# Four PSUM banks for the second layer's sums, three for the first layer, one GpSimd block to a step, and four slots for g_full

## The chip, the cores and the metric

The kernel runs on one core of one Trainium2 chip. The metric is the time of one execution on the device, in microseconds (us). Three runs of the kernel before took 740.76, 741.46 and 741.74 us; their median is 741.46 us.

## What is computed

The reference is a "macaron" block: a feed-forward half (FFN), a gated linear recurrence (the mixer) and the same feed-forward half once more, on 8 sequences of 1024 rows with 256 features, all in float32. Cut to what matters:

```python
def ffn(x):                                   # x: (8, 1024, 256)
    h = layernorm(x) * gamma + beta
    y = silu(h @ dequant(fc1_q, fc1_scales) + fc1_bias)    # 256 -> 1024, scales by groups of 128 rows
    z = y @ dequant(fc2_q, fc2_scales) + fc2_bias          # 1024 -> 256
    return x + 0.5 * z
def mixer(x):
    a, c = sigmoid(x @ Wa + ba), tanh(x @ Wc + bc)
    b, d = x @ Wb + bb, x @ Wd + bd
    s[t] = a[t] * s[t-1] + (1 - a[t]) * b[t]               # over the rows of a sequence
    return (c * s) @ Wy + by + d
x = x + 0.5 * ffn(ln(x));  x = x + mixer(ln(x));  x = x + 0.5 * ffn(ln(x))
```

## The kernel before

The 8192 rows are cut into 16 tiles of 512 rows. The whole of x stays on chip in `resid`. Three phases follow each other: 16 tiles of the first FFN, 16 of the mixer, 16 of the second FFN. An FFN tile has eight steps, f = 0 to 7, one for each block of 128 hidden features. Every engine (PE is TensorE, ACT ScalarE, DVE VectorE, POOL GpSimd) runs its own list of instructions in program order, written out by hand step by step, and semaphores tie the lists together. In step f of a tile the engines do this:

- PE (`feed_forward` from L963): `half_products(f)` (two matmuls, the first 128 input features, into a bank of `ps_fc1`), `fc2` n = 0 of the group four steps back (two matmuls into a bank of `ps_z`; `LAG` is 4), `add_products(f-1)` (two matmuls, the other 128 input features, onto the half that has been scaled in place), `fc2` n = 1. In two of the steps (`TURN_AT`) `turn` (L889) follows, four transposes that bring one half of the next tile's `xhat` into `ps_tr`; in two others (`TURN_BACK_AT`) `turn_back` (L950), four transposes that bring z back. The two matmuls of a pair take the rounded value and its remainder (`h_hi` and `h_lo`, or `g_hi` and `g_lo`).
- ACT (from L574): `scale_half` for the f in `SCALED_ON_ACT`, `silu(f-1)` (the same bank read twice, into `g_full` and into `g_hi`), `round_h` after a turn, `first_sum` for the two sums of group 0, and one block of the layer norm (`normalise`, the block in `REST`) in step 7.
- DVE (from L702): `scale_half` for the other f, `add_group` (two additions of a PSUM bank onto `z_acc`, for groups 1 to 7), `lower_h` after a turn, `add_ffn` after a turn back, statistics (`STATISTICS_AT`) and variance.
- POOL (from L440): `g_low(f-1)` (L393: `g_lo` = `g_full` - `g_hi`) first in every step. Then, by tile position, `residual` (L384, four blocks that scale the next tile's `resid`), `rsqrt` (L342 to L366) for the tile after the next, and `normalise` (L374, three blocks of that tile's `xhat`; after the last one `xhat_ready` is raised).

The constants at L36 to L52 are tuples indexed by `before`, that is 0, 1 or 2 for tile 0, tile 1 and every later tile. In tiles 2 to 15 POOL does `residual` in step 1, `rsqrt` in step 2, `normalise` in steps 5 (two blocks) and 6 (one block); PE turns in steps 1 and 3 of the following tile. `turn(ln, ...)` waits for `xhat_ready` to reach ln + 1, and PE's whole list waits behind it. There is one `xhat` buffer and one `ps_tr` bank for the turns.

PSUM has eight banks of 128x512 float32. `ps_fc1` has four, used in turn (f % 4), so `half_products(f)` waits for `g_hi` of f - 4. `ps_z` has three, and the 16 sums of a tile go through them in turn (`BANKS`, L33), so a sum waits until the sum three before it has been added (`filled_before`, L244). `ps_tr` has one. `g_full` has two slots, so `silu(g)` waits for `g_low(g-2)` (L559); `g_hi` and `g_lo` have four slots and wait for `fc2` of g - 4.

## Time and profile before

| quantity | value |
|---|---|
| median of three runs | 741.46 us |
| the profiled execution | 739.66 us |
| its span, first to last instruction | 737.8 us |
| granted TensorE clock, mean | 0.998 |
| PE / PEld / DVE busy | 698.3 / 539.9 / 627.5 us |
| ACT / POOL busy | 637.0 / 623.6 us |
| busiest group on POOL: `g_lo` L393, 256 times | 329.5 us, 1293 ns each |
| busiest group on DVE: `z_acc` L690, 448 times | 322.5 us, 747 ns each |

PE counts the matmuls, PEld the loads of their weights, which overlap the matmuls. "Busy" is the time in which an engine had an instruction under way. The profiled execution lasted 1.86 us longer than its span, and its time is 1.8 us below the median of the three runs. The phases follow each other in the trace: the first FFN until about 305 us, the mixer until about 440 us, the second FFN until the end. In a timeline a line is: start in us, duration in us, engine, source line, operation, output<-inputs, shapes, count. Starts of neighbouring instructions may overlap, because the engines are pipelined; the distance between two starts is what an instruction costs its engine.

### The profile page before, as it was taken

To read this page: it belongs to the slowest core of one execution; us is meant where nothing else is said; L and a number is where in the kernel's file an instruction comes from. 1 tells how busy PE (TensorE), PEld (TensorE's weight loads), DVE (VectorE), ACT (ScalarE), POOL (GpSimd) and SP (SyncE) were. 2 spreads that over 40 slices of the span, in tenths; PEclk is the share of its full clock that TensorE was granted. 3 is DMA by queue.
4 is the path that set the end of the run, shared out by engine and by line. 5 is a ranking of instruction groups with operands and counts; after the bars stand their busy time and mean duration, and the time that the engine had idled before them with its cause. 6 is when DMAs were issued, how large, how long until landed. Compare 5 with 4: busy or idle time off the path is not lost. (4 is left out here: it accounts for less than half of the span.)

```text
span 737.8 us, 13716 instructions
## 1 busy us (share of the span) xinstructions
PE 698.3 (95%) x3250; PEld 539.9 (73%) x3250; DVE 627.5 (85%) x1216; ACT 637.0 (86%) x1052; POOL 623.6 (85%) x800
## 2 busy tenths in 40 slices
PE   4899999999999999989999997999999999999996
PEld 3577777777777777767788874777777777777774
DVE  6599998999999988688777785999999998999886
ACT  4889899998998999688888878889999899998984
POOL 5899999999999988767666658999999999999963
PEclk9999999999999999999999999999999999999999
DMA  8640000000000000000000000001110000000001
GB/s 259 205 140 1 1 0 0 0 0 0 0 0 0 1 1 0 1 1 1 0 0 0 1 0 1 2 28 35 44 37 28 28 29 28 28 30 28 30 30 59
DMA packets 19674, 19.96 MB, mean 27 GB/s; under 512 B 1532, under 2 KB 19378, under 8 KB 19634
## 3 DMA queue, kind: packets, MB, share of 16 engines
q1 hardware_dynamic: 19536, 19.48, 8.3%
q8 instruction: 16, 0.26, 0.1%
q14 instruction: 24, 0.20, 0.1%
q10 hardware_dynamic: 98, 0.02, 0.0%
HBM read 11.11 MB, written 8.39 MB: 26 GB/s over the span
## 5 line engine op out<-in xcount | busy, mean ns | idle before, releaser
L690 DVE SCALAR_TENSOR_TENSOR z_acc<-ps_z,cols,z_acc 128x512 f32<-128x512 f32 x448 | 322.5, 747 | 55.2 <-PE ps_z L902 24.5
L393 POOL TENSOR_TENSOR g_lo<-g_full,g_hi 128x512 fp32r<-128x512 f32 x256 | 329.5, 1293 | 36.2 <-ACT g_hi L562 35.4
L902 PE MATMUL ps_z<-g_hi,q_sb 128*128 128x512 f32 x512 | 210.8, 412 | 16.1 <-ACT z_acc L552 8.4
L560 ACT ACTIVATE g_full<-ps_fc,safe_scale 128x512 f32<-128x512 f32 x256 | 178.6, 698 | 51.9 <-PE ps_fc L902 38.6
L902 PE MATMUL ps_fc<-h_hi,q_sb 128*128 128x512 f32 x512 | 215.1, 420 | 4.8 <-ACT ps_fc L545 4.1
L902 PE MATMUL ps_fc<-h_lo,q_sb 128*128 128x512 f32 x512 | 203.6, 398 | 0.0
L902 PE MATMUL ps_z<-g_lo,q_sb 128*128 128x512 f32 x512 | 202.1, 395 | 0.0
L562 ACT ACTIVATE g_hi<-ps_fc,safe_scale 128x512 fp32r<-128x512 f32 x256 | 178.5, 697 | 0.0
L902 PEld LDWEIGHTS ps_z<-g_hi,q_sb 128*128 128x128 f32 x512 | 96.0, 187 | 69.5 <-ACT z_acc L552 22.4
L545 ACT ACTIVATE ps_fc<-ps_fc,bias,ratio 128x512 f32<-128x512 f32 x160 | 122.2, 764 | 1.4 <-DVE bias L785 1.4
L902 PEld LDWEIGHTS ps_fc<-h_hi,q_sb 128*128 128x128 f32 x512 | 97.2, 190 | 25.8 <-ACT ps_fc L545 4.1
L902 PEld LDWEIGHTS ps_z<-g_lo,q_sb 128*128 128x128 f32 x512 | 96.4, 188 | 19.1
L902 PEld LDWEIGHTS ps_fc<-h_lo,q_sb 128*128 128x128 f32 x512 | 97.6, 191 | 17.2
L670 DVE TENSOR_SCALAR ps_fc<-ps_fc,ratio,bias 128x512 f32<-128x512 f32 x96 | 77.9, 811 | 4.5 <-PE ps_fc L902 4.5
L360 POOL TENSOR_TENSOR rstd<-var_terms,minus_half 128x8 f32<-128x8 f32 (+1 forms) x48 | 69.6, 1451 | 4.0
L384 POOL TENSOR_SCALAR resid<-resid,res_scale,shift 128x256 f32<-128x256 f32 x128 | 69.3, 555 | 0.8 <-ACT xhat L528 0.8
L651 DVE BATCH_NORM_STATS2 stats<-resid 128x6 f32 (+1 forms) x192 | 67.0, 410 | 1.8 <-DMA resid<-in_L_attn_x 1.8
L1018 PE MATMUL ps_fc<-wd_sb,q_int 128*128 128x256 f32 x240 | 56.7, 379 | 0.0
L528 ACT ACTIVATE xhat<-resid,shift,rstd 128x256 f32 (+1 forms) x96 | 52.2, 591 | 4.0 <-POOL shift L366 3.9
L374 POOL TENSOR_SCALAR xhat<-resid,rstd,shift 128x256 f32<-128x256 f32 x96 | 53.4, 562 | 0.1
L895 PE MATMUL ps_tr<-ident,xhat 128*128 128x128 f32 x320 | 48.6, 275 | 3.0 <-ACT xhat L528 1.5
L895 PEld LDWEIGHTS ps_tr<-ident,xhat 128*128 128x128 f32 x320 | 39.6, 141 | 14.9 <-issue 4.0
(105 smaller groups left out, 813.8 us busy)
## 6 DMA issues: line engine op xcount, KB each, us to landing
resid<-in_L_attn_x SPq DMA_DIRECT2D x15, 512.0 KB, 4.2
out_x<-resid SPq DMA_DIRECT2D x15, 512.0 KB, 2.9
q_int<-in_L_ffn_fc_q SPq DMA_DIRECT2D x4, 512.0 KB, 7.0
...
```

Of the source, the lines that this page charges most:

```text
L360: nc.gpsimd.tensor_tensor(rstd[:, 0:n, :], var_terms[:, 0:n, :], minus_half[:, 0:n, :], ALU.pow).then_inc(rstd_ready, 1)
L384: last = nc.gpsimd.tensor_scalar(resid[:, t, a, :], resid[:, t, a, :], res_scale[:, a:a + 1], shift[:, 1, a:a + 1], ALU.mult, ALU.add)
L393: nc.gpsimd.tensor_tensor(g_lo[:, g % 4, :], g_full[:, g % 2, :], g_hi[:, g % 4, :].bitcast(F32), ALU.subtract).then_inc(g_ready, 1)
L545: nc.scalar.activation(bank, bank, ACT.Identity, bias=bias[:, f:f + 1], scale=ratio[:, f:f + 1]).then_inc(scaled_on_act, 1)
L560: nc.scalar.activation(g_full[:, g % 2, :], bank, ACT.Silu, scale=scale)
L562: nc.scalar.activation(g_hi[:, g % 4, :], bank, ACT.Silu, scale=scale).then_inc(g_hi_ready, 1)
L651: last = nc.vector.bn_stats(stats[:, a, :], resid[:, t, a, :])
L670: nc.vector.tensor_scalar(bank, bank, ratio[:, f:f + 1], bias[:, f:f + 1], ALU.mult, ALU.add).then_inc(scaled_on_dve, 1)
L690: nc.vector.scalar_tensor_tensor(out=z, in0=bank_of(g, n, par), scalar=col(R_S2 + KC * g + n), in1=z, op0=ALU.mult, op1=ALU.add).then_inc( ...
L895: last = nc.tensor.transpose(bank[:, a * P:(a + 1) * P], xhat[:, a, c * P:(c + 1) * P], ident[:, :])
L902: last = nc.tensor.matmul(out, w, v, start=start and i == 0, stop=stop and i == len(pairs) - 1, skip_group_check=not start)
L1018: nc.tensor.matmul(mix_bank(t, par, half)[:, a * D:(a + 1) * D], xn[:, par, k, at:at + P], wd_sb[:, k, :], start=False, stop=False, skip_g ...
```

## The change

`ps_fc1` gets three banks and `ps_z` four. The sums of the second layer use bank 2 * (g % 2) + n, so a sum waits for the addition of group g - 2 with the same n. The first layer's banks follow the list `FC1_BANKS`; where a bank comes again after two steps (f = 1 of even tiles, f = 7 of odd tiles), `half_products` is issued after `add_products` (`HALF_LATE`). `g_full` gets four slots. The constants move work between steps: POOL's four `residual` blocks go to steps 0 to 3, `rsqrt` to step 4, the three `normalise` blocks to steps 5, 6 and 7; PE's turns of tiles 2 to 15 go to steps 0 and 2, its turns back to 4 and 5, with `round_h`, `lower_h` and `add_ffn` moved to match; the variance goes to step 7; ACT scales f = 1, 3, 5, 6, 7 and DVE f = 0, 2, 4; both first sums are issued in step 4. No arithmetic is added or removed. The mixer's banks get other numbers. The diff, cut to its core:

```diff
-    BANKS = tuple(tuple((FC * KC * par + KC * g + n) % 3 for g in range(FC)) for par in range(2) for n in range(KC))
-    SCALED_ON_ACT = (0, 2, 4, 5, 6)
-    SCALED_ON_DVE = (1, 3, 7)
+    FC1_BANKS = (0, 1, 2, 0, 1, 2, 0, 1, 2, 0, 1, 2, 0, 1, 2, 1)
+    HALF_LATE = ((1,), (7,))
+    SCALED_ON_ACT = (1, 3, 5, 6, 7)
+    SCALED_ON_DVE = (0, 2, 4)
     TINY = 2.0 ** -60
     STATISTICS_AT = 4
-    VARIANCE_AT = 5
-    RESIDUAL_AT = (4, 1, 1)
-    RSQRT_AT = (5, 2, 2)
-    NORMALISE_AT = ((6, 7), (5, 6), (5, 6))
-    TURN_AT = ((3, 5), (1, 3), (1, 3))
-    TURN_OUT_AT = ((3, 5), (1, 3), (1, 3))
-    H_LOWER_AT = ((4, 6), (2, 4), (2, 4))
-    XN_LOWER_AT = (4, 6)
-    FIRST_SUM_AT = (4, 5)
-    TURN_BACK_AT = ((), (5, 6), (5, 6))
-    ADD_AT = ((), (6, 7), (6, 7))
+    VARIANCE_AT = 7
+    RESIDUAL_AT = ({2: (0, 1), 3: (2, 3)},) + ({0: (0,), 1: (1,), 2: (2,), 3: (3,)},) * 2
+    RSQRT_AT = (5, 4, 4)
+    NORMALISE_AT = ({6: (0, 1), 7: (2,)},) + ({5: (0,), 6: (1,), 7: (2,)},) * 2
+    TURN_AT = ((3, 5), (1, 3), (0, 2))
+    TURN_OUT_AT = ((3, 5), (1, 3), (0, 2))
+    H_LOWER_AT = ((4, 6), (2, 4), (1, 3))
+    XN_LOWER_AT = (3, 5)
+    TURN_BACK_AT = ((), (5, 6), (4, 5))
+    ADD_AT = ((), (6, 7), (5, 6))
...
-        g_full = sb("g_full", [P, 2, TILE])
+        g_full = sb("g_full", [P, 4, TILE])
...
-        ps_fc1 = ctx.enter_context(nc.psum_tensor("ps_fc1", [P, 4, TILE], F32))
-        ps_z = ctx.enter_context(nc.psum_tensor("ps_z", [P, 3, TILE], F32))
+        ps_fc1 = ctx.enter_context(nc.psum_tensor("ps_fc1", [P, 3, TILE], F32))
+        ps_z = ctx.enter_context(nc.psum_tensor("ps_z", [P, 4, TILE], F32))
         ps_tr = ctx.enter_context(nc.psum_tensor("ps_tr", [P, TILE], F32))
-        ps_tr2 = ps_z[:, 2, :]
+        ps_tr2 = ps_z[:, 3, :]
         back_banks = (ps_tr[:, :], ps_fc1[:, 0, :])
-        ps_ab = ps_z[:, 0, :]
-        ps_c = ps_z[:, 1, :]
+        ps_ab = ps_z[:, 1, :]
+        ps_c = ps_z[:, 2, :]
+        ps_mix = ((ps_fc1[:, 0, :], ps_fc1[:, 2, :]), (ps_fc1[:, 1, :], ps_z[:, 0, :]))
...
+        def fc1_bank(f, par):
+            return ps_fc1[:, FC1_BANKS[FC * par + f], :]
+        def silu_before(f, par):
+            here = FC * par + f
+            return next(k for k in range(1, FC) if FC1_BANKS[here - k] == FC1_BANKS[here])
+        def bank_of(g, n):
+            return ps_z[:, KC * (g % 2) + n, :]
+        def filled_before(g, n, ff):
+            if g == 2:
+                return z_begun[n], ff + 1
+            if g > 2:
+                return z_added[n], (FC - 1) * ff + (g - 2)
+            return z_added[n], (FC - 1) * ff + (g - 1)
...
+            def normalise(ln, t, blocks, complete):
                 if blocks[0] == 0:
                     pool.wait_ge(shift_ready, ln + 1)
@@ -373,24 +382,26 @@
                 for a in blocks:
                     last = nc.gpsimd.tensor_scalar(xhat[:, a, :], resid[:, t, a, :], rstd[:, 0, a:a + 1],
                                                    shift[:, 0, a:a + 1], ALU.mult, ALU.add)
-                if last_part:
+                if complete:
                     last.then_inc(xhat_ready, 1)
-            def residual(ln, t, shares):
-                pool.wait_ge(xhat_ready, ln + 1)
-                wait(pool, xhat_half_ready, shares)
-                for a in range(SUB):
+            def residual(ln, t, shares, blocks=range(SUB)):
+                if blocks[0] == 0:
+                    pool.wait_ge(xhat_ready, ln + 1)
+                    wait(pool, xhat_half_ready, shares)
+                for a in blocks:
                     last = nc.gpsimd.tensor_scalar(resid[:, t, a, :], resid[:, t, a, :], res_scale[:, a:a + 1],
                                                    shift[:, 1, a:a + 1], ALU.mult, ALU.add)
-                last.then_inc(resid_scaled, 1)
+                if blocks[-1] == SUB - 1:
+                    last.then_inc(resid_scaled, 1)
...
-                        if behind >= 1 and f == RESIDUAL_AT[before]:
-                            residual(ln + 1, t + 1, share(ln + 1, ff0))
+                        if behind >= 1 and f in residual_at:
+                            residual(ln + 1, t + 1, share(ln + 1, ff0), residual_at[f])
                         if behind >= 2 or ff0 == 0:
                             t2, twice = (t + 2, True) if behind >= 2 else (1 - behind, False)
                             if f == RSQRT_AT[before]:
                                 rsqrt(ln + 2, twice, share(ln + 1, ff0))
                             if f in normalise_at:
-                                normalise(ln + 2, t2, MOST[normalise_at.index(f)], f == normalise_at[1])
+                                normalise(ln + 2, t2, normalise_at[f], f == FC - 1)
...
-                wait(act, g_ready, FC * ff + (g - 1))
-                nc.scalar.activation(g_full[:, g % 2, :], bank, ACT.Silu, scale=scale)
+                wait(act, g_ready, FC * ff + (g - 3))
+                nc.scalar.activation(g_full[:, g % 4, :], bank, ACT.Silu, scale=scale)
...
-                        if f == FIRST_SUM_AT[1]:
-                            first_sum(ff, par, 1)
                         if f in SCALED_ON_ACT:
-                            scale_half(ff, f)
+                            scale_half(ff, f, par)
+                        if f == LAG:
+                            first_sum(ff, par, 0)
                         if f >= 1:
                             silu(ff, f - 1, par)
...
-                        if f == FIRST_SUM_AT[0]:
-                            first_sum(ff, par, 0)
+                        if f == LAG:
+                            first_sum(ff, par, 1)
...
-                wait(pe, g_hi_ready, FC * ff + (f - 3))
-                products(ps_fc1[:, f % 4, :], [(w[:, 0, f * P:(f + 1) * P], h[:, par, 0, :])
+                wait(pe, g_hi_ready, FC * ff + (f + 1 - silu_before(f, par)))
+                products(fc1_bank(f, par), [(w[:, 0, f * P:(f + 1) * P], h[:, par, 0, :])
...
-                        half_products(ff, ln, f, par)
+                        if f not in HALF_LATE[par]:
+                            half_products(ff, ln, f, par)
...
+                        if f in HALF_LATE[par]:
+                            half_products(ff, ln, f, par)
```

## Rows read from the trace of the kernel before

**Rows 1.** Page, busy time by engine, and the last chain by line.

```profile
PE 698.3 (95%) x3250; PEld 539.9 (73%) x3250; DVE 627.5 (85%) x1216; ACT 637.0 (86%) x1052; POOL 623.6 (85%) x800
...
POOL g_lo L393 14%; POOL rstd L360 3%; POOL resid L384 3%; POOL xhat L374 3%; PE ps_z L902 2%; PE ps_fc L902 2%; DVE z_acc L690 0%; POOL neg_mean L357 0%; POOL var_terms L353 0%; POOL var_terms L351 0%; PE ps_tr L959 0%; POOL shift L366 0%;
```

**Rows 2.** Windows over tiles 2 to 14; columns: stretch, length, engines, clock, DMA.

```profile
56.60:268.91 212.31, 207.45 (x961) 160.64 (x960) 193.80 (x361) 193.36 (x316) 197.92 (x252) 1.00 0.00 0
484.21:695.97 211.76, 207.27 (x961) 160.76 (x960) 191.81 (x352) 192.65 (x313) 198.19 (x253) 1.00 0.09 30
```

**Rows 3.** Timeline of PE, one steady tile of the second FFN.

```profile
474.25 0.40 PE L902 MATMUL ps_fc<-h_lo,q_sb 128*128 128x512 f32 x1
474.91 0.50 PE L902 MATMUL ps_z<-g_hi,q_sb 128*128 128x512 f32 x1 [0.27 <-ACT z_acc L552]
475.25 0.40 PE L902 MATMUL ps_z<-g_lo,q_sb 128*128 128x512 f32 x1
...
476.16 0.39 PE L902 MATMUL ps_fc<-h_lo,q_sb 128*128 128x512 f32 x1
...
477.03 0.40 PE L902 MATMUL ps_z<-g_lo,q_sb 128*128 128x512 f32 x1
...
479.32 0.40 PE L902 MATMUL ps_z<-g_lo,q_sb 128*128 128x512 f32 x1
...
483.51 0.40 PE L902 MATMUL ps_fc<-h_lo,q_sb 128*128 128x512 f32 x1
```

**Rows 4.** Timeline of PE: turns (tiles 1, 2, 14, mixer; then 1, 2, 14).

```profile
38.95 0.66 PE L895 MATMUL ps_tr<-ident,xhat 128*128 128x128 f32 x4
...
56.60 0.60 PE L895 MATMUL ps_tr<-ident,xhat 128*128 128x128 f32 x4
...
268.91 0.60 PE L895 MATMUL ps_tr<-ident,xhat 128*128 128x128 f32 x4
...
303.62 0.60 PE L895 MATMUL ps_tr<-ident,xhat 128*128 128x128 f32 x4
...
466.59 0.63 PE L895 MATMUL ps_tr<-ident,xhat 128*128 128x128 f32 x4
...
484.21 0.60 PE L895 MATMUL ps_tr<-ident,xhat 128*128 128x128 f32 x4
...
695.97 0.60 PE L895 MATMUL ps_tr<-ident,xhat 128*128 128x128 f32 x4
```

**Rows 5.** Timeline of POOL, the same steady tile.

```profile
471.11 1.31 POOL L393 TENSOR_TENSOR g_lo<-g_full,g_hi 128x512 fp32r<-128x512 f32 x1
...
475.35 2.54 POOL L393 TENSOR_TENSOR g_lo<-g_full,g_hi 128x512 fp32r<-128x512 f32 x2
...
480.42 1.30 POOL L393 TENSOR_TENSOR g_lo<-g_full,g_hi 128x512 fp32r<-128x512 f32 x1
481.71 0.56 POOL L374 TENSOR_SCALAR xhat<-resid,rstd,shift 128x256 f32<-128x256 f32 x1
482.23 1.30 POOL L393 TENSOR_TENSOR g_lo<-g_full,g_hi 128x512 fp32r<-128x512 f32 x1
```

**Rows 6.** Timelines of ACT and POOL: the way to POOL, and first_sum.

```profile
484.03 0.69 ACT L560 ACTIVATE g_full<-ps_fc,safe_scale 128x512 f32<-128x512 f32 x1 [0.23 <-PE ps_fc L902]
484.61 0.68 ACT L562 ACTIVATE g_hi<-ps_fc,safe_scale 128x512 fp32r<-128x512 f32 x1
...
485.37 1.29 POOL L393 TENSOR_TENSOR g_lo<-g_full,g_hi 128x512 fp32r<-128x512 f32 x1 [0.20 <-ACT g_hi L562]
...
491.94 1.45 ACT L552 ACTIVATE z_acc<-ps_z,cols 128x512 f32<-128x512 f32 x2
```

**Rows 7.** Timeline of POOL, the shorter rsqrt of tile 14, first FFN.

```profile
273.69 1.29 POOL L393 TENSOR_TENSOR g_lo<-g_full,g_hi 128x512 fp32r<-128x512 f32 x1
...
276.86 2.53 POOL L393 TENSOR_TENSOR g_lo<-g_full,g_hi 128x512 fp32r<-128x512 f32 x2
```

**Rows 8.** Window with PE idle, start of second FFN (columns as rows 2).

```profile
448.00:450.00 2.00, 0.08 (x1) 0.08 (x1) 1.96 (x7) 1.85 (x4) 2.00 (x4) 1.00 0.00 0
```

More of the change, by code:

```diff
@@ L57, in macaron_kernel @@
     out_view = out.rearrange("b s d -> (b s) d").rearrange("(t a p) d -> p t a d", p=P, a=SUB)
-    MOST, REST = (range(0, 2), range(2, 3)), range(3, 4)
+    REST = (3,)
     R_S1, R_B1 = 0, KC * FC
@@ L133, in macaron_kernel @@
         xn_hi, xn_lo = h_hi, h_lo
-        c_sb, state = g_full[0:N, :, :], z_acc[0:N, 0, :, :]
+        c_sb, state = g_full[0:N, 0:2, :], z_acc[0:N, 0, :, :]
         scratch = q1_int[:, :, :].bitcast(F32).rearrange("p k f -> p (k f)").rearrange("p (b n) -> p b n", n=TILE)
@@ L239, in scaled_count @@
             return len(where) * ff + (where.index(f) + 1)
-        def bank_of(g, n, par):
-            return ps_z[:, BANKS[2 * par + n][g], :]
-        def filled_before(bank, g, n, ff, par):
-            here = [(j, m) for j in range(FC) for m in range(KC)]
-            before = here[:here.index((g, n))] if g < FC else here
-            for back, uses, p in ((0, before, par), (1, here, 1 - par)):
-                for j, m in reversed(uses):
-                    if BANKS[2 * p + m][j] == bank:
-                        if j == 0:
-                            return z_begun[m], ff - back + 1
-                        return z_added[m], (FC - 1) * (ff - back) + j
+        def fc1_bank(f, par):
[11 more added lines that the diff above has]
+            return z_added[n], (FC - 1) * ff + (g - 1)
         def share(ln, ff0):
@@ L264, in mix_bank @@
             if type(t) is int and t == NT - 1:
-                return ps_z[:, half, :]
-            return ps_fc1[:, 2 * par + half, :]
+                return ps_z[:, 1 + half, :]
+            return ps_mix[par][half]
         halves = (range(0, SUB // 2), range(SUB // 2, SUB))
@@ L551, in first_sum @@
                 wait(act, back_done, 2 * ff - 2)
-                nc.scalar.activation(z_acc[:, par, n, :], bank_of(0, n, par), ACT.Identity,
+                nc.scalar.activation(z_acc[:, par, n, :], bank_of(0, n), ACT.Identity,
                                      bias=col(R_B2 + n), scale=col(R_S2 + n)).then_inc(z_begun[n], 1)
             def silu(ff, g, par):
-                step, bank, scale = FC * ff + g, ps_fc1[:, g % 4, :], safe_scale[:, g:g + 1]
+                step, bank, scale = FC * ff + g, fc1_bank(g, par), safe_scale[:, g:g + 1]
                 act.wait_ge(fc1_done, step + 1)
-                wait(act, g_ready, FC * ff + (g - 1))
-                nc.scalar.activation(g_full[:, g % 2, :], bank, ACT.Silu, scale=scale)
+                wait(act, g_ready, FC * ff + (g - 3))
+                nc.scalar.activation(g_full[:, g % 4, :], bank, ACT.Silu, scale=scale)
                 wait(act, fc2_done, 2 * step - 6)
@@ L668, in scale_half @@
                     dve.wait_ge(bias_ready, 1)
-                bank = ps_fc1[:, f % 4, :]
+                bank = fc1_bank(f, par)
                 nc.vector.tensor_scalar(bank, bank, ratio[:, f:f + 1], bias[:, f:f + 1], ALU.mult,
@@ L936, in fc2 @@
                     pe.wait_ge(g_ready, FC * ff + (g + 1))
-                bank = bank_of(g, n, par)
-                wait(pe, *filled_before(BANKS[2 * par + n][g], g, n, ff, par))
+                bank = bank_of(g, n)
+                wait(pe, *filled_before(g, n, ff))
                 at = slice(n * P, (n + 1) * P)
```

31 lines of the change are left out of this document (14 added, 17 removed).

## The prediction, made before the result was known

> **What bounds the kernel now.** I read the page's busy times first, then windows, then the timeline of one steady tile. No engine stands out: PE has 95%, the other three 85 or 86% [rows 1]. The chain that ended last runs through POOL more than through any other engine, mostly `g_lo` [rows 1]. The windows give the rate. In the second FFN the first turns of tiles 2 and 14 are 211.76 us apart [rows 2, 4], so 12 tiles take 17.65 us each; in the first FFN it is 17.69. In one such tile PE is busy 17.3 us, POOL 16.5, ACT 16.1 and DVE 16.0 (rows 2 divided by 12). For PE that number says little, because the shown durations overlap; I count issue slots. From 479.32 to 483.51 there are 18 slots, 0.233 us each. Four transposes cost 0.44 us: 475.25 to 476.16 is 0.91 and holds two slots beside them [rows 3]. A tile has 64 products and four groups of transposes: 64 x 0.233 + 4 x 0.44 = 16.7 us. So PE loses 0.95 us per tile, in small waits on banks and on `g_lo`. Between 474.25 and 475.25 it loses 1.00 - 0.47 = 0.53 us, waiting for a first sum; between 476.16 and 477.03 another 0.40 [rows 3].
>
> **The order that matters here: xhat to turn.** In the kernel before, the last POOL block of `xhat` ends at 482.27 (start 481.71, 0.56 us) and the first turn of the next tile starts at 484.21 [rows 4, 5]. The turn is 1.94 us later than it would have to be. That block stands in POOL's step 6 and the turn at the end of PE's step 1. The change puts them in POOL's step 7 and at the end of PE's step 0: two steps of PE nearer, 2 x 8 x 0.233 = 3.7 us and a group of transposes where one lies between. 1.9 us of slack can't pay for that. This decides the forecast, so I work out the loop that it closes.
>
> **The new loop.** Let a tile's first turn start at 0. PE's list from there to the end of `add_products(3)` in step 4 is fixed: the turn (0.44), steps 1, 2 and 3 with 24 products, the second turn (0.44), and in step 4 `half_products(4)`, `fc2` and `add_products(3)`, 6 products: 30 x 0.233 + 0.88 = 7.9 us. Nothing can overtake, as the list is in order. ACT then has to finish `first_sum(0)`, which it now issues before `silu(3)`: it can start two slots (0.47) before the end of `add_products(3)` and takes 0.73 (1.45 for two, rows 6), so it adds some 0.2. From a finished `add_products` to the start of `g_low` on POOL it takes 1.6 us: the last product's slot ends at 483.74, `silu` is read twice by ACT, and `g_lo` starts at 485.37 [rows 3, 6]. So POOL starts `g_low(3)` at 9.7. Behind it in POOL's list stand `rsqrt`, now in step 4, then `g_low(4)`, a block, `g_low(5)`, a block, `g_low(6)`, the last block. From `g_lo` through `rsqrt` to the next `g_lo` POOL takes 475.35 - 471.11 = 4.24 us, and a `g_lo` with one block takes 482.23 - 480.42 = 1.81 [rows 5]: 4.24 + 3 x 1.81 + 0.1 for the end of the last block and the signal = 9.8. The next turn can't start before 9.7 + 9.8 = 19.5; I take 19.4, since `silu` was reached a little late in the row used. PE by itself would be there at 16.7, so it stands still for 2.7 us in each tile, at one place. All its small waits are hidden in that one.
>
> **The edits, one by one.** (1) Four `ps_z` banks and the earlier `first_sum` take away the waits on z sums, part of the 0.95 us; with PE stalled 2.7 us elsewhere they give nothing in tiles 2 to 14 and about 0.5 us in each tile where no turn waits. (2) Three `ps_fc1` banks: `half_products(f)` now waits for `silu(f-3)`, which by the 1.6 us above is done about a step before. Cost nothing while ACT has room, which it has (16.1 of 19.4 us). (3) The two late `half_products` give the scaling on ACT less time: it starts two product pairs later, and `silu` behind it starts up to 0.7 us later. It falls on f = 1 or 7, not on the path through `silu(3)`; nothing. (4) Four slots of `g_full` take ACT's wait for POOL away. That wait holds ACT up behind POOL's `rsqrt` now; in the loop above no ACT wait is left to remove. (5) `residual` one block to a step: the same four blocks; they lie before `g_low(3)`, where POOL has time. `g_low` and a block take 1.81 us a step and PE's steps 1.87 or 2.3, so `g_low(3)` isn't late. (6) The moved turns back, `add_ffn`, variance and DVE's scalings: DVE has 16.0 us of work in 19.4 and each addition waits for PE; nothing. The one tight place is the second turn, two steps behind the first, which needs `lower_h` of the first; these stood two steps apart before too, and the distance is the same. I allow 0 to 0.3 us a tile there. Before these edits no row shows a tile with a turn that waits, so the bounds of the per-tile cost are the one-path value of the second rival below (+0.15) and 19.4 + 0.3 (+2.05); I take 19.4, as each of its terms is a measured distance.
>
> **The sum,** on the profiled execution. First FFN: tile 0 has its `residual` earlier, which can save POOL up to 1 us before its last `xhat` block; I take 0.5, so the first turn of tile 1 moves from 38.95 [rows 4] to 38.4. That turn stays in step 1, one step (1.87) later in the list than in later tiles: to the first turn of tile 2 it is 19.4 - 1.87 = 17.6 us, at 56.0. Then 12 intervals of 19.4: tile 14's turn at 288.8, where it was at 268.91. `rsqrt` of tiles 14 and 15 has fewer operations: from `g_lo` to `g_lo` 276.86 - 273.69 = 3.17 [rows 7], 1.07 less, so tile 15's turn comes 18.3 later. Tile 15's own `xhat` has two `xn_low` of about 1.3 us (as a `g_lo`) between the `g_low`s, of which one and a half lie on the path: 20.3. The mixer's first turn comes at 327.4 in place of 303.62 [rows 4]: +23.8. The mixer keeps its work and order; a bank wait at its start goes, -0.4. Second FFN: tile 1's turn from 466.59 to 466.59 + 23.4 - 0.7 = 489.3, tile 2's at 506.9, tile 14's 232.8 later at 739.7, where it was at 695.97: +43.7. From there to the end PE runs unstalled; it has one step more to do (+1.9) and loses three small waits (-1.5). Together +44 us: the profiled execution goes from 739.66 to about 783.8, and the median, which lies 1.8 above it, from 741.46 to 785.5.
>
> **Rivals.** (a) The change does what its parts are for: no turn waits, the z waits are gone, and the tile falls to what POOL and PE need, 16.85 us. That gives 25 x 0.8 + 4 = 24 us less, 717. It is faster, and decides if `xhat` is complete 2.7 us earlier than I work out, that is if `rsqrt` and the three blocks lie beside PE's steps 5 to 0. For it: POOL's 16.5 us fit. Against it: even without `rsqrt`, the last block needs `add_products(6)` of step 7, 1.6 us to POOL, a `g_lo` and a block: 1.4 + 1.6 + 1.81 = 4.8 us after step 7 began, and the turn is due after 3.7. (b) The loop closes only by that last path: `rsqrt` is absorbed, and a tile takes 16.7 + 1.1 = 17.8 us: +0.15 a tile, 25 tiles and 1.3 us at the start of each FFN give 747. Against it is that POOL's list has no way around `rsqrt`. (c) PE's stall of 2.7 us brings the clock down to its lower level behind each stall: with 4 us of a tile's path at half speed, 2 us more a tile, 835. Against it: PE stood still for nearly all of 448 to 450 us and the granted clock read 1.00 [rows 8]; it is 1.00 in the steady stretches too [rows 2]. (d) Small waits add up to 0.5 us a tile in the loop: 797.
>
> The Trainium skill's page "TensorE: Matmul & The Clock Gate", section "HAM oscillation — how this bites in real kernels", says that a matmul engine with long enough idle gaps goes back to the throttled clock; by it rival (c) would hold if the gaps here were long enough, and the row of 448 to 450 us doesn't show it. The page "Perfetto Trace Analysis", section "Optimization Strategy", says that the same gap coming back on the engine that should be saturated can mean too little PSUM for the next tile; by it the fourth `ps_z` bank is the cure and rival (a) the outcome. PE's wait for a first sum agrees with it, but the fourth bank doesn't reach the new wait.
>
> **How the numbers follow.** Forecast 785.5 with chance 0.79; (a) 0.06, (b) 0.04, (c) 0.03, (d) 0.08. Uncertainty of the forecast itself: 0.35 us a tile over 25 tiles is 9 us, and 3 us for the starts and ends, so 773 to 798, which takes in (d); this is the range for 8 in 10. A change of 0.2% is 1.5 us, about what a measurement can tell from none. Faster is (a), 0.06; within 0.2% 0.01; slower 0.93.
>
> **What would show it.** If right: first turns of tiles 2 to 14 are 19.4 us apart; PE idle for 2.5 to 3 us just before each, released by POOL's `xhat`; POOL without idle time from `g_low(3)` to the last block; no PE wait on `z_acc` in these tiles. Three loop terms can be read off alone: 7.9, 1.8 and 9.8. If turns start without a wait, or the tile takes less than 17.7 us, the loop is wrong. If the tile is longer than 19.8, look at `lower_h` before the second turn, or at the clock.

## The result, and the profile after

The changed kernel took 813.47 us (median of four runs, 813.15 to 813.73) beside 741.6 us before: a ratio of 1.097, with a 95% interval of 1.0951 to 1.0989. It is slower, as forecast, but by 72 us where 44 were forecast, and it lies 15.5 us above the upper end of the range. The profiled execution took 813.32 us, with a span of 811.5 us.

The page of the changed kernel: busy time by engine, then the chain that ended last, by engine and by line.

```profile
PE 718.2 (89%) x3250; PEld 557.2 (69%) x3250; DVE 626.9 (77%) x1216; ACT 643.0 (79%) x1052; POOL 624.9 (77%) x800
...
PE 22%; POOL 13%; issue 5%; DVE 1%; POOLq 0%; DVEq 0%; ACT 0%
PE ps_z L913 9%; PE ps_fc L913 9%; POOL g_lo L404 6%; POOL xhat L383 2%; PE ps_tr L906 2%; POOL rstd L369 2%; POOL resid L394 1%; PE ps_tr L970 1%; POOL neg_mean L366 0%; POOL shift L375 0%; POOL var_terms L360 0%; POOL var_terms L362 0%; D
```

POOL and DVE are as busy as before in us (624.9 and 626.9), and less in share; PE shows 20 us more than in [rows 1], for the same 3250 instructions. Two things are to be seen already: no engine has more work, so time was lost in waits, and something made the same matmuls longer.

The windows over tiles 2 to 14 of both FFNs, from first turn to first turn (stretch and length; busy us and count for PE, PEld, DVE, ACT, POOL; granted clock; DMA share):

```profile
58.33:304.76 246.43, 218.37 (x961) 169.97 (x961) 191.88 (x360) 196.04 (x315) 198.43 (x252) 0.94 0.00 0
523.29:769.01 245.72, 216.54 (x960) 168.81 (x961) 190.55 (x351) 195.18 (x312) 198.47 (x253) 0.95 0.08 26
```

Twelve tiles take 246.43 and 245.72 us where [rows 2] has 212.31 and 211.76: 20.5 us a tile. And the granted clock is 0.94 and 0.95, where it was 1.00. A mean hides how that is spread, so I read the first turns one by one. The timeline of PE, three first turns that follow each other (start, duration, engine, line, output<-inputs, shapes, count, and in brackets the idle time before it with its releaser):

```profile
160.64 1.03 PE L906 MATMUL ps_tr<-ident,xhat 128*128 128x128 f32 x4 [2.49 <-POOL xhat L383]
...
181.75 0.65 PE L906 MATMUL ps_tr<-ident,xhat 128*128 128x128 f32 x4 [2.21 <-POOL xhat L383]
...
201.28 0.73 PE L906 MATMUL ps_tr<-ident,xhat 128*128 128x128 f32 x4 [2.48 <-POOL xhat L383]
```

PE stands still 2.2 to 2.5 us before each, and POOL's `xhat` ends it, as forecast. But the intervals are 21.11 and 19.53 us, and these are the two kinds there are: of the 24 intervals between tile 2 and tile 14 in the two FFNs, 9 are 19.5 to 19.7 us and 15 are 20.8 to 21.2 us. The windows of one us just after a turn of a long interval, and just after one of a short interval, show the difference (columns as above):

```profile
161.00:162.00 1.00, 1.00 (x6) 0.90 (x5) 0.00 (x0) 0.21 (x1) 1.00 (x2) 0.50 0.00 0
162.00:163.00 1.00, 1.00 (x4) 0.81 (x3) 0.00 (x0) 0.92 (x2) 0.28 (x1) 0.50 0.00 0
163.00:164.00 1.00, 1.00 (x3) 0.75 (x3) 0.49 (x1) 0.32 (x1) 0.00 (x0) 0.50 0.00 0
164.00:165.00 1.00, 1.00 (x5) 0.83 (x4) 0.49 (x2) 0.65 (x2) 0.00 (x0) 0.91 0.00 0
165.00:166.00 1.00, 1.00 (x6) 0.79 (x5) 1.00 (x2) 0.62 (x2) 0.30 (x1) 1.00 0.00 0
...
182.00:183.00 1.00, 1.00 (x8) 0.87 (x7) 0.01 (x1) 0.47 (x1) 1.00 (x2) 1.00 0.00 0
183.00:184.00 1.00, 1.00 (x6) 0.82 (x5) 0.74 (x1) 0.38 (x2) 0.41 (x1) 1.00 0.00 0
```

After the turn at 160.64 the granted clock is 0.50, the lower of the two levels (1.2 GHz), until about 164; after the turn at 181.75 it is 1.00. Each of the 15 long intervals has such a stretch at its start, 3.4 us long when it is read in half-microsecond windows, and none of the 9 short ones has one. The products under it start 0.43 us apart in place of 0.233:

```profile
162.32 0.63 PE L913 MATMUL ps_z<-g_hi,q_sb 128*128 128x512 f32 x1
162.75 0.63 PE L913 MATMUL ps_z<-g_lo,q_sb 128*128 128x512 f32 x1
163.18 0.63 PE L913 MATMUL ps_fc<-h_hi,q_sb 128*128 128x512 f32 x1
```

The loop of the prediction can be checked in the short interval. The timeline of POOL between the turns at 181.75 and 201.28, its end left out:

```profile
185.86 1.29 POOL L404 TENSOR_TENSOR g_lo<-g_full,g_hi 128x512 fp32r<-128x512 f32 x1 [2.44 <-ACT g_hi L573]
...
191.50 1.28 POOL L404 TENSOR_TENSOR g_lo<-g_full,g_hi 128x512 fp32r<-128x512 f32 x1
192.88 0.20 POOL L360 TENSOR_SCALAR var_terms<-mean_var 128x4 f32<-128x4 f32 x1
...
193.68 1.64 POOL L369 TENSOR_TENSOR rstd<-var_terms,minus_half 128x8 f32<-128x8 f32 x1
...
195.72 1.29 POOL L404 TENSOR_TENSOR g_lo<-g_full,g_hi 128x512 fp32r<-128x512 f32 x1
197.01 0.56 POOL L383 TENSOR_SCALAR xhat<-resid,rstd,shift 128x256 f32<-128x256 f32 x1
197.54 1.28 POOL L404 TENSOR_TENSOR g_lo<-g_full,g_hi 128x512 fp32r<-128x512 f32 x1
198.82 0.55 POOL L383 TENSOR_SCALAR xhat<-resid,rstd,shift 128x256 f32<-128x256 f32 x1
199.35 1.26 POOL L404 TENSOR_TENSOR g_lo<-g_full,g_hi 128x512 fp32r<-128x512 f32 x1
200.60 0.55 POOL L383 TENSOR_SCALAR xhat<-resid,rstd,shift 128x256 f32<-128x256 f32 x1
```

`g_low(3)` starts at 191.50, 9.75 us after the turn (forecast 9.7). From there POOL has no gap to speak of: to the `g_lo` behind `rsqrt` 4.22 us (4.24), then three times `g_lo` and a block, and the next turn starts at 201.28, 9.78 us after `g_low(3)` (9.8). In the long interval before it, `g_low(3)` comes here:

```profile
171.95 1.30 POOL L404 TENSOR_TENSOR g_lo<-g_full,g_hi 128x512 fp32r<-128x512 f32 x1
```

That is 11.31 us after its turn: 1.56 more, and then 9.80 again to 181.75. So the lower clock costs 1.56 us in PE's part of this loop, and nothing in POOL's. Over all 24 intervals the long ones average 1.5 us more than the short ones.

### The profile page after: what moved, and what is told of

Read it like the earlier page. It is cut to its first block and busy times, and to the rows that moved or that the text cites. A ratio compares the mean times of both kernels' runs of the same rounds, so it can differ in the third digit from the quotient of the medians.

```text
span 811.5 us, 13584 instructions
## 1 busy us (share of the span) xinstructions
PE 718.2 (89%) x3250; PEld 557.2 (69%) x3250; DVE 626.9 (77%) x1216; ACT 643.0 (79%) x1052; POOL 624.9 (77%) x800
## 3 DMA queue, kind: packets, MB, share of 16 engines
q1 hardware_dynamic: 19536, 19.48, 7.5%
## 5 line engine op out<-in xcount | busy, mean ns | idle before, releaser
L913 PE MATMUL ps_fc<-h_hi,q_sb 128*128 128x512 f32 x512 | 223.4, 436 | 3.4 <-DVE ps_fc L681 3.2
L913 PE MATMUL ps_fc<-h_lo,q_sb 128*128 128x512 f32 x512 | 209.6, 409 | 0.0
L913 PE MATMUL ps_z<-g_lo,q_sb 128*128 128x512 f32 x512 | 206.0, 402 | 0.0
L913 PEld LDWEIGHTS ps_fc<-h_hi,q_sb 128*128 128x128 f32 x512 | 101.7, 199 | 34.3 <-ACT g_hi L573 7.8
L913 PEld LDWEIGHTS ps_z<-g_hi,q_sb 128*128 128x128 f32 x512 | 100.0, 195 | 27.9 <-POOL g_lo L404 3.3
L906 PE MATMUL ps_tr<-ident,xhat 128*128 128x128 f32 x320 | 55.1, 300 | 72.1 <-POOL xhat L383 61.2
L913 PEld LDWEIGHTS ps_z<-g_lo,q_sb 128*128 128x128 f32 x512 | 99.6, 194 | 22.4
L913 PEld LDWEIGHTS ps_fc<-h_lo,q_sb 128*128 128x128 f32 x512 | 101.8, 199 | 17.9
L531 ACT ACTIVATE h_hi<-ps_tr,cols 128x512 fp32r<-128x512 f32 x62 | 42.9, 693 | 60.1 <-PE ps_tr L906 60.1
L394 POOL TENSOR_SCALAR resid<-resid,res_scale,shift 128x256 f32<-128x256 f32 x128 | 71.7, 562 | 0.8 <-ACT xhat L539 0.8
```

The lines of the kernel that those rows point to most:

```text
L394: last = nc.gpsimd.tensor_scalar(resid[:, t, a, :], resid[:, t, a, :], res_scale[:, a:a + 1], shift[:, 1, a:a + 1], ALU.mult, ALU.add)
L906: last = nc.tensor.transpose(bank[:, a * P:(a + 1) * P], xhat[:, a, c * P:(c + 1) * P], ident[:, :])
L913: last = nc.tensor.matmul(out, w, v, start=start and i == 0, stop=stop and i == len(pairs) - 1, skip_group_check=not start)
```

## The experiments

"Loop theory" is the prediction's: the tile is the closed way from turn to `g_low(3)`, through POOL's list, to the next turn. "Clock theory" was formed from the result: the loop gives 19.5, and the rest of the miss is the lower clock behind each stall. Each ratio is to the kernel before on the same chip (739.93 to 740.72 us in these sessions), with its 95% interval.

**The turns back in steps 1 and 3.** All else stays as changed.

```diff
-    TURN_AT = ((3, 5), (1, 3), (0, 2))
+    TURN_AT = ((3, 5), (1, 3), (1, 3))
...
-    H_LOWER_AT = ((4, 6), (2, 4), (1, 3))
-    XN_LOWER_AT = (3, 5)
-    TURN_BACK_AT = ((), (5, 6), (4, 5))
-    ADD_AT = ((), (6, 7), (5, 6))
+    H_LOWER_AT = ((4, 6), (2, 4), (2, 4))
+    XN_LOWER_AT = (4, 6)
+    TURN_BACK_AT = ((), (5, 6), (5, 6))
+    ADD_AT = ((), (6, 7), (6, 7))
```

> The changed kernel with one part undone: PE's turns of tiles 2 to 15 are back in steps 1 and 3 (with round_h, lower_h, turn_back and add_ffn moved with them); banks, slots and POOL's order stay as changed. Theory (the loop turn, add_products(3), rsqrt, three blocks, turn): the turn stands 1.87 us later in PE's list, so the part of the loop that PE takes is that much shorter, and a tile takes 19.5 - 1.9 = 17.7 us. PE stands still about 0.9 us before a turn instead of 2.5, and the granted clock stays at 1.00. Median 742 (736 to 748). Rival (the three ps_fc1 banks and the late halves cost the time): the tile stays above 19 us and the median above 790.

Measured: 742.78 us, ratio 1.003 [1.002, 1.0039]. The timelines of PE and of POOL in this kernel:

```profile
147.95 0.65 PE L906 MATMUL ps_tr<-ident,xhat 128*128 128x128 f32 x4 [0.63 <-POOL xhat L383]
...
165.64 0.65 PE L906 MATMUL ps_tr<-ident,xhat 128*128 128x128 f32 x4
...
183.31 0.65 PE L906 MATMUL ps_tr<-ident,xhat 128*128 128x128 f32 x4 [0.65 <-POOL xhat L383]
...
155.84 1.29 POOL L404 TENSOR_TENSOR g_lo<-g_full,g_hi 128x512 fp32r<-128x512 f32 x1 [0.67 <-ACT g_hi L573]
```

One step less of PE's list between turn and `g_low(3)` (1.87 us) takes the loop to 17.6, and the turns are 17.69 and 17.67 us apart. The kernel before has tiles of 17.65 to 17.69 us too, for other reasons [rows 2], so the time alone doesn't show the loop. The rows do: `g_low(3)` starts at 155.84, 7.89 us after the turn (7.8 by the forecast's terms less one step), and from there POOL runs on without a gap to the turn at 165.64, 9.80 us later. The wait before a turn is 0.6 to 0.8 us or none, where 0.9 was expected, and the clock is 0.996. Putting the turns back takes away 71 of the 72 us. That doesn't make it the price of the early turns alone, as a later experiment shows: they need `rsqrt` in step 4 and the last block in step 7 to cost so much.

**PE kept busy while it waits.** Ten matmuls are put ahead of the turn's wait for `xhat`, into the bank that the turn then overwrites.

```diff
...
+                for i in range(filler):
+                    nc.tensor.matmul(bank[:, :], q1_sb[:, 0, 0:P], q1_sb[:, 0, 0:TILE], start=True, stop=True)
...
+                                 filler=10 if before == 2 and f == 0 else 0)
```

> The changed kernel with ten added 128x512 matmuls (their result is overwritten) on PE just before the first turn of each tile from tile 2 on, ahead of the wait for xhat: 10 x 0.233 = 2.3 us of work inside the 2.5 us in which PE stood still. The loop is as it was. Theory (the tiles of 21.1 us are tiles of 19.55 us in which the matmul clock fell after the idle time): granted clock 1.00 throughout, all steady tiles 19.5 to 19.7 us, median 791 (787 to 796). Rival (the 21.1 us tiles come from something else, such as the late halves or a wait on DVE): the pattern stays and the median is 813 or more.

Measured: 792.06 us, ratio 1.0693 [1.0675, 1.0711]: 21.4 us less than the changed kernel, with more work on PE. The window over the first FFN:

```profile
58.00:300.00 242.00, 240.94 (x1122) 189.48 (x1121) 198.41 (x370) 202.62 (x327) 204.65 (x260) 1.00 0.00 1
```

The clock reads 1.00, and all twelve intervals of the first FFN are 19.39 to 19.48 us, those of the second 19.4 to 19.7. The long kind is gone. The useful work of PE still waits for `xhat` as it did, so this separates the two losses: the wait itself, and what the clock does after it.

**Less filler.** The same with four matmuls, so that some 1.2 to 1.7 us of idle time stays.

```diff
-                                 filler=10 if before == 2 and f == 0 else 0)
+                                 filler=4 if before == 2 and f == 0 else 0)
```

> The changed kernel with four added matmuls ahead of the wait for xhat in place of ten: 0.9 us of the 2.5 us idle is filled, 1.6 us stays. In the runs so far idle gaps of up to 1.7 us before a turn left the clock at its full level, gaps of 2.2 us and more were followed by the lower level in more than half of the tiles. Theory (the length of the idle gap decides): clock 1.00, all steady tiles 19.5 us, median 791 (789 to 794). Rival (PE's share of idle time over a longer stretch decides): some tiles of 21 us remain, median 796 to 812.

Measured: 790.29 us, ratio 1.0678 [1.066, 1.0695]; the clock over the same window is 1.00 again. With 1.2 to 1.7 us idle before a turn in place of 2.2 to 2.6 the clock falls behind no turn. The filler shortens each gap and PE's idle time as a whole together, so the run doesn't tell which of the two counts.

**`rsqrt` early.** The turns stay early; `rsqrt` goes back to step 2, the `residual` blocks to steps 0 and 1, two to a step.

```diff
-    RESIDUAL_AT = ({2: (0, 1), 3: (2, 3)},) + ({0: (0,), 1: (1,), 2: (2,), 3: (3,)},) * 2
-    RSQRT_AT = (5, 4, 4)
+    RESIDUAL_AT = ({2: (0, 1), 3: (2, 3)},) + ({0: (0, 1), 1: (2, 3)},) * 2
+    RSQRT_AT = (5, 2, 2)
```

> The changed kernel with rsqrt back in POOL's step 2 and the residual blocks two each in steps 0 and 1, ahead of it; turns stay in steps 0 and 2, the xhat blocks in 5, 6 and 7. Theory: two paths into the turn are left, both near 17.8 us: through add_products(1), rsqrt, five g_low and three blocks (5.3 + 4.24 + 2.6 + 5.5 = 17.7), and through add_products(6), g_low(6) and the last block, 1.1 us after the turn is due (16.7 + 1.1 = 17.8). PE stands still 1.1 us before a turn, clock 1.00, median 747 (740 to 754). Rival (rsqrt's place doesn't matter, as the last block in step 7 by itself sets the wait of 2.5 us): about as long as the changed kernel, above 785.

Measured: 772.94 us, ratio 1.0437 [1.042, 1.0454], where 747 was expected. A tile takes 18.73 us or 18.99, not 17.8. The timelines of PE and POOL from one turn to the next:

```profile
172.27 0.65 PE L906 MATMUL ps_tr<-ident,xhat 128*128 128x128 f32 x4 [1.67 <-POOL xhat L383]
...
191.00 0.65 PE L906 MATMUL ps_tr<-ident,xhat 128*128 128x128 f32 x4 [1.33 <-POOL xhat L383]
...
176.38 1.29 POOL L404 TENSOR_TENSOR g_lo<-g_full,g_hi 128x512 fp32r<-128x512 f32 x1 [1.93 <-ACT g_hi L573]
177.65 1.10 POOL L394 TENSOR_SCALAR resid<-resid,res_scale,shift 128x256 f32<-128x256 f32 x2
178.70 1.30 POOL L404 TENSOR_TENSOR g_lo<-g_full,g_hi 128x512 fp32r<-128x512 f32 x1
...
182.94 3.79 POOL L404 TENSOR_TENSOR g_lo<-g_full,g_hi 128x512 fp32r<-128x512 f32 x3
186.72 0.56 POOL L383 TENSOR_SCALAR xhat<-resid,rstd,shift 128x256 f32<-128x256 f32 x1
...
190.31 0.56 POOL L383 TENSOR_SCALAR xhat<-resid,rstd,shift 128x256 f32<-128x256 f32 x1
```

The loop closes elsewhere. From the turn at 172.27 it is 4.1 us to `g_low(0)`, which waited 1.93 us for ACT; from there POOL runs without a gap through two blocks, `g_low(1)`, `rsqrt`, three `g_low`, and the rest, to the last block at 190.31. 4.1 + 14.5 + 0.1 = 18.7. I had let the path join POOL's list at `g_low(6)` and had taken what stands before it as done beside PE. It isn't: once `g_low(0)` waits for the turn, all of POOL's tile stands behind that turn. In the changed kernel that longer way was already there and nearly as long: after the turn at 181.75 `g_low(0)` starts 4.11 us later, at 185.86, and from there to the end of the last block POOL takes 15.3 us, of which 0.2 are gaps. With 0.1 for the signal and without the gaps that is 19.4 us, against the 19.5 of the way through `g_low(3)`, so moving `rsqrt` out of the one way could take off little.

**The early turns alone,** in the kernel before.

```diff
-    TURN_AT = ((3, 5), (1, 3), (1, 3))
+    TURN_AT = ((3, 5), (1, 3), (0, 2))
...
-    H_LOWER_AT = ((4, 6), (2, 4), (2, 4))
-    XN_LOWER_AT = (4, 6)
+    H_LOWER_AT = ((4, 6), (2, 4), (1, 3))
+    XN_LOWER_AT = (3, 5)
-    TURN_BACK_AT = ((), (5, 6), (5, 6))
-    ADD_AT = ((), (6, 7), (6, 7))
+    TURN_BACK_AT = ((), (5, 6), (4, 5))
+    ADD_AT = ((), (6, 7), (5, 6))
```

> The kernel before with PE's turns in steps 0 and 2 and the turns back in 4 and 5 (round_h, lower_h and add_ffn moved with them), nothing else; POOL's last xhat block stays in step 6. In the kernel before xhat is there 1.94 us ahead of the turn, and the turn comes 1.87 us sooner. Theory: just no wait, or one of 0.1 to 0.2 us in a tile: median 742 (738 to 747), so the early turns cost only together with the last block in step 7 and rsqrt in step 4. Rival (the moved turns back, add_ffn and lower_h cost DVE or PE something by themselves): above 750.

Measured: 750.71 us, ratio 1.0145 [1.0128, 1.0162], where 742 was expected. The timelines of PE and POOL:

```profile
145.89 0.66 PE L895 MATMUL ps_tr<-ident,xhat 128*128 128x128 f32 x4 [0.30 <-POOL xhat L374]
...
164.09 0.66 PE L895 MATMUL ps_tr<-ident,xhat 128*128 128x128 f32 x4 [0.32 <-POOL xhat L374]
...
149.41 1.30 POOL L393 TENSOR_TENSOR g_lo<-g_full,g_hi 128x512 fp32r<-128x512 f32 x1 [1.15 <-ACT g_hi L562]
150.69 2.17 POOL L384 TENSOR_SCALAR resid<-resid,res_scale,shift 128x256 f32<-128x256 f32 x4
...
163.40 0.56 POOL L374 TENSOR_SCALAR xhat<-resid,rstd,shift 128x256 f32<-128x256 f32 x1
```

It is the same loop: turn at 145.89, `g_low(0)` 3.5 us later after a wait for ACT, then POOL's list almost without a gap (one wait of 0.19 us) to the last block at 163.40, and the turn at 164.09, 18.2 us after the first. I had compared only the slack of 1.94 us between last block and turn [rows 4, 5] with the 1.87 us of a step. The slack was spent within one tile, but the next tile's POOL list then started later too, and nothing gave that back. So the early turns cost some 11 us in the old order; the rest of the 71 comes from what the change put between `g_low(3)` and the last block.

**The banks alone.** The changed kernel with POOL's steps, variance and turns as before; what stays is the banks, the slots, the late halves, the scaling on ACT and DVE and the earlier first sums.

```diff
-    RESIDUAL_AT = ({2: (0, 1), 3: (2, 3)},) + ({0: (0,), 1: (1,), 2: (2,), 3: (3,)},) * 2
-    RSQRT_AT = (5, 4, 4)
-    NORMALISE_AT = ({6: (0, 1), 7: (2,)},) + ({5: (0,), 6: (1,), 7: (2,)},) * 2
-    TURN_AT = ((3, 5), (1, 3), (0, 2))
+    RESIDUAL_AT = ({4: (0, 1, 2, 3)},) + ({1: (0, 1, 2, 3)},) * 2
+    RSQRT_AT = (5, 2, 2)
+    NORMALISE_AT = ({6: (0, 1), 7: (2,)},) + ({5: (0, 1), 6: (2,)},) * 2
+    TURN_AT = ((3, 5), (1, 3), (1, 3))
...
```

> The banks and slots of the change alone (four ps_z, three ps_fc1 with the late halves and the new split of the scaling, four g_full, both first sums in step 4), with the steps of POOL's blocks, of the turns and of the variance as in the kernel before. Theory: xhat has its 1.9 us of slack again, the waits on z sums and of ACT for g_low are gone, and the tile goes down to what POOL and PE need, 16.8 to 17.0 us: median 722 (716 to 728). Rival (rsqrt in one piece holds POOL's g_lo back and PE waits for it as often as before): the tile stays at 17.4 to 17.7 us and the median at 735 to 742.

Measured: 758.52 us, ratio 1.0243 [1.0226, 1.026], where 722 was expected, and outside what its rival gave too: a loss in place of a gain. The waits of this kernel from 60 to 280 us (engine, line, releaser: us in total, times, longest):

```profile
PEld ps_z L913 <- POOL g_lo L404: 17.8, 12, 1.8
...
PE ps_z L913 <- POOL g_lo L404: 12.5, 12, 1.3
...
PEld ps_fc L913 <- ACT g_hi L573: 6.1, 6, 1.9
PE ps_fc L913 <- ACT g_hi L573: 3.4, 6, 1.4
```

No wait for a bank of `ps_z` is left, so the fourth bank did what it is for. In their place PE waits for `g_lo`, up to 1.8 us at a time, and for `g_hi` where a half is late. Intervals are 18.25 and 18.36 us. In this trace the `g_lo` that PE waits for stands behind POOL's lump of four `residual` blocks and `rsqrt`. Why the tile is longer than in the kernel before, which has the same lump, isn't shown: three `ps_fc1` banks, late halves, the new split of the scaling and the earlier first sums all came in together. The Trainium skill, page "Perfetto Trace Analysis", section "Optimization Strategy", says that a gap repeating on the engine that should be saturated can mean too little PSUM for the next tile. This run agrees with it as far as the waits on z sums go, which are gone with the fourth bank, and not on the time, which grew; but the bank was taken from the first layer, so no run here shows what a bank more would do.

**Four slots of `g_full` alone,** in the kernel before.

```diff
-        g_full = sb("g_full", [P, 2, TILE])
+        g_full = sb("g_full", [P, 4, TILE])
...
-                wait(act, g_ready, FC * ff + (g - 1))
+                wait(act, g_ready, FC * ff + (g - 3))
```

> The kernel before with four slots of g_full in place of two, nothing else. ACT no longer waits for POOL's g_lo (0.5 us in each tile). Theory: that wait passed POOL's rsqrt on to ACT and from there to PE, so part of POOL's idle time (0.7 us a tile) goes: 17.3 to 17.5 us a tile, median 735 (731 to 739). Rival (the wait was hidden, since PE waits on z banks anyway): median 739 to 742, no difference to the kernel before.

Measured: 740.59 us, ratio 1.0004 [0.9994, 1.0014]. 735 was expected. ACT's waits for `g_lo` (12 of them, 5.6 us in all from 60 to 280 us in the kernel before) are gone from the list of waits, and PE's waits are what they were. The slots are worth nothing here.

**`rsqrt` in step 3.** The first experiment, with `rsqrt` one step earlier.

```diff
-    RESIDUAL_AT = ({2: (0, 1), 3: (2, 3)},) + ({0: (0,), 1: (1,), 2: (2,), 3: (3,)},) * 2
-    RSQRT_AT = (5, 4, 4)
+    RESIDUAL_AT = ({2: (0, 1), 3: (2, 3)},) + ({0: (0, 1), 1: (2,), 2: (3,)},) * 2
+    RSQRT_AT = (5, 3, 3)
```

> As the run with the turns back in steps 1 and 3, and rsqrt one step earlier too (POOL's step 3; the residual blocks two in step 0, one each in steps 1 and 2). Theory of the loop: from the turn to add_products(2) PE takes 0.4 + 1.9 + 0.4 + 1.4 = 4.1 us, 1.6 us to POOL, then 4.24 + 1.3 + 3 x 1.81 + 0.1 = 11.1: 16.8 us a tile, down from 17.7, so that PE, POOL and the loop all want 16.7 to 17.0. Median 724 (718 to 730). Rival (the late half_products hold ACT's silu and so POOL's g_low back by 0.8 to 1.9 us a tile, whatever stands where on POOL): 17.5 us or more a tile, median 737 to 745.

Measured: 727.08 us, ratio 0.9817 [0.9801, 0.9833]. With `rsqrt` out of the way between `g_low(3)` and the last block, no turn of tiles 2 to 14 waits any more; tiles take 16.65 and 17.55 us in turn. The longer ones hold a wait of up to 1.4 us on `g_hi`, at the late half.

**`silu` ahead of the scaling at the late half,** on top of that.

```diff
...
-                        if f in SCALED_ON_ACT:
+                        if f in SCALED_ON_ACT and f not in HALF_LATE[par]:
...
+                        if f in SCALED_ON_ACT and f in HALF_LATE[par]:
+                            scale_half(ff, f, par)
```

> As the run with rsqrt in step 3 and turns in steps 1 and 3, and in the two steps with a late half_products ACT issues silu(f-1) ahead of scale_half(f), so that silu doesn't wait for the late half. Theory: POOL gets g_low(0) of even tiles and g_low(6) of odd tiles 0.7 to 1.3 us earlier, while add_products(f) in the next step waits for the scaling, about 0.3 us on PE. If the late halves are what holds the run without this order back, this one is faster than it by 5 to 15 us; if the loop through rsqrt alone sets the tile, it is the same within 2 us or slower by up to 8 (the 0.3 us on PE).

Measured: 724.66 us, ratio 0.9786 [0.977, 0.9802]. It takes 2.4 us off, which lies between the two cases expected (5 us or more, or at most 2), and the intervals remain 16.65 and 17.55. The late half costs something by making `silu` wait; that isn't the whole of the difference to the next kernel.

**The old banks with the new order.** The kernel before with four `ps_fc1` banks and three of `ps_z`, turns in steps 1 and 3, POOL's blocks as in the last two kernels, four slots, and the first sum issued ahead of `silu(3)`.

```diff
-    VARIANCE_AT = 5
-    RESIDUAL_AT = (4, 1, 1)
-    RSQRT_AT = (5, 2, 2)
-    NORMALISE_AT = ((6, 7), (5, 6), (5, 6))
+    VARIANCE_AT = 7
+    RESIDUAL_AT = ({2: (0, 1), 3: (2, 3)},) + ({0: (0, 1), 1: (2,), 2: (3,)},) * 2
+    RSQRT_AT = (5, 3, 3)
+    NORMALISE_AT = ({6: (0, 1), 7: (2,)},) + ({5: (0,), 6: (1,), 7: (2,)},) * 2
-    FIRST_SUM_AT = (4, 5)
+    FIRST_SUM_AT = 4
...
```

> The kernel before with its banks (four for the first layer, three for z, no late half), its turns in steps 1 and 3 and its split of the scaling, but with four slots of g_full, POOL's blocks spread (residual in steps 0, 0, 1, 2, rsqrt in 3, xhat in 5, 6, 7), the variance in step 7 and both first sums in step 4, the first ahead of silu(3). Theory: the change's gain lies in POOL's spread order and the slots, and its loss in the early turns and the late halves; without these two a tile takes 16.9 to 17.2 us, median 725 (718 to 731). Rival (PE's waits on three z banks bind once POOL is spread): 17.5 us a tile and no gain, median 736 to 744.

Measured: 719.16 us, ratio 0.9717 [0.9701, 0.9733]; only the next kernel is as fast. Its window over tiles 2 to 14 of the first FFN, first turn to first turn:

```profile
55.60:258.84 203.24, 202.15 (x961) 161.69 (x961) 190.87 (x361) 191.54 (x316) 197.38 (x252) 1.00 0.00 0
```

16.94 us a tile (203.24 / 12), where the count of PE's slots gives 16.7; POOL is busy for 97% of it. It is also 5.5 us faster than the last kernel. Those two kernels differ in the banks of both layers, the late half and in who scales which f, and I haven't taken these apart: together, what comes with three `ps_fc1` banks costs more than the fourth `ps_z` bank gives.

**Two slots in this kernel.** `g_full` as before the change.

```diff
-                wait(act, g_ready, FC * ff + (g - 3))
+                wait(act, g_ready, FC * ff + (g - 1))
...
```

> As the run with the old banks and POOL's work spread (719.2 us), but with two slots of g_full. ACT's silu then waits for g_low(g-2) again, and with POOL busy the whole tile and up to 2 us behind after rsqrt, ACT is held up with it, and PE's add_products stand behind that. Theory (the slots were useless alone because POOL's lumps and the z waits covered them, and are needed once POOL is the bound): 17.2 to 17.5 us a tile, median 732 (726 to 738). Rival (the slots never matter): 719 to 721.

Measured: 719.34 us, ratio 0.9721 [0.9704, 0.9737]. 732 was expected. Even here the slots don't matter.

**The first sums in their old places,** on top of that; what is left of the edits is POOL's order and the variance.

```diff
-                        if f == FIRST_SUM_AT:
-                            first_sum(ff, par, 0)
+                        if f == FIRST_SUM_AT[1]:
+                            first_sum(ff, par, 1)
...
```

> The kernel before with its banks and its two slots, and POOL's order alone changed (residual in steps 0, 0, 1, 2, rsqrt in 3, xhat in 5, 6, 7, variance in 7): the first sums are back behind silu(3) and in step 5, as in the kernel before. Theory (a PE with 16.7 us of work in a tile of 16.9 has no room for the 0.5 us wait on the first sum): 17.2 to 17.4 us a tile, median 730 (726 to 735), and the earlier first sum is worth some 10 us. Rival (the wait on the first sum was a late effect of POOL's lumps and goes with them): 719 to 722.

Measured: 732.18 us, ratio 0.9897 [0.9881, 0.9914]. The waits from 60 to 280 us:

```profile
PEld ps_z L904 <- ACT z_acc L554: 8.4, 13, 0.7
...
PE ps_z L904 <- ACT z_acc L554: 2.7, 13, 0.3
```

These are the waits for a first sum, as the kernel before has them; in the kernel with the earlier first sums PE has none. So of the 21 us that the best kernel gains, POOL's order gives 8, and the earlier first sums give 13 more on top of it, with three banks of `ps_z` both times: PE's waits for a first sum went without a fourth bank. What the earlier first sums give without POOL's new order wasn't run.

## Why the prediction was right in direction and wrong in size

**What held.** Direction, place and releaser of the stall held. The loop's terms measured 9.75, 4.22 and 9.78 us for 9.7, 4.24 and 9.8, and the tile at full clock is 19.5 to 19.7 us against a worked-out 19.5, of which I took 19.4. No turn started without a wait in tiles 2 to 14, the idle time before it is 2.1 to 2.6 us for 2.7, and the turn of tile 15 comes 18.38 us after that of tile 14 for 18.3. Rival (a) needed `xhat` 2.7 us earlier, and rival (b) a way around `rsqrt`; neither happened. The small waits of rival (d) hardly appeared: at full clock a tile is 19.5 us in the first FFN and 19.6 in the second. With the turns put back the loop theory gave the time to 1 us.

**Where the 29.5 us went.** The forecast of the profiled execution was 783.8, it took 813.3. By stretches: tile 2's turn of the first FFN came at 58.33, not 56.0 (+2.3); the twelve tiles to tile 14 took 246.4 for 232.8 (+13.6); tile 15 and the mixer's turn came +0.75; the mixer and the start of the second FFN -0.3; its twelve tiles 245.7 for 232.8 (+12.9); the end +0.2.

**The step that failed** is the price of the clock. The sum takes the tile of 19.4 us at full clock and puts the clock's fall behind PE's stall at nothing; it stands only in rival (c), with 3 in 100 and 835 us, "2 us more a tile" in each tile. The evidence against it was one window of the kernel before in which PE stood still for nearly all of 2 us at a clock of 1.00 [rows 8], and the 1.00 of steady stretches that hold no such stall [rows 2]. One stretch without a fall was taken for a rule. In truth 15 of 24 intervals lost 1.5 us each in the mean, in all 22 of the 26.5 us that the two rows of twelve tiles went over. The run with PE kept busy shows it on its own: those 24 intervals sum to 468.6 us in it, 23.6 fewer than in the changed kernel, and its 792.06 us would have lain in the range. The right case was between the forecast and (c): the loop with part of the tiles at the lower clock, and a range to 798 left it out. The Trainium skill, page "TensorE: Matmul & The Clock Gate", section "HAM oscillation — how this bites in real kernels", says that long enough idle gaps bring the engine back to the throttled clock; with the fall to 0.50 behind gaps of 2.2 to 2.6 us this trace agrees. The waits of the page's own example are longer than these; that gaps of this length can do it, and in part of the tiles only, is what these rows add.

**Smaller terms.** The rest of the 26.5 us, some 4, is the 0.1 to 0.2 us between the 19.4 that I took and the 19.5 to 19.7 that came; the terms had added up to 19.5. The start was +2.3: tile 1's turn came at 40.72, where 38.4 was forecast and the kernel before had 38.95. The trace shows where. In tile 0 the half of f = 0 is now scaled by DVE, which starts on it at 18.35, where ACT started at 17.28 before, and PE's list stands 2.19 us behind it:

```profile
17.28 0.75 ACT L545 ACTIVATE ps_fc<-ps_fc,bias,ratio 128x512 f32<-128x512 f32 x1 [1.42 <-DVE bias L785]
...
18.35 0.82 DVE L681 TENSOR_SCALAR ps_fc<-ps_fc,ratio,bias 128x512 f32<-128x512 f32 x1 [0.42 <-issue]
...
19.32 0.77 PE L913 MATMUL ps_fc<-h_hi,q_sb 128*128 128x512 f32 x1 [2.19 <-DVE ps_fc L681]
```

(The first line is of the kernel before, the others of the changed one.) The late half of f = 1 comes behind that, and ACT scales it before `silu(0)`, so POOL's first `g_lo` starts at 23.42 in place of 20.75. The earlier `residual` by itself saved little: with the old banks and the old split tile 1's turn is at 38.72.

**Costs I set at nothing.** The three `ps_fc1` banks, the late half and the new split of the scaling were "nothing"; in the steady tiles the stall hid them. Without it, they or the parts that came with them cost: 758.5 us against 740.7 with the old order, and 724.7 against 719.2 with the good one. The early turns alone (742 expected, 750.7 measured) and the early `rsqrt` (747, 772.9) show a weakness in how rival (b) was reckoned: I had closed the loop at one place and not looked for the longest of all ways around.

**What stays open.** Why the clock falls behind 15 of 24 nearly equal gaps and not behind the other 9. The length of the gap doesn't tell them apart: it is 2.17 to 2.58 us before a fall and 2.19 to 2.59 without one. Nor is it known which of banks, late half and scaling makes up the last 5.5 us, or the 18 us of the banks alone.
